# One MoE-plus-state-space layer kernel on one core: order of work in three stages changed

## The reference

```python
xn = layernorm(x)                                   # no gain or offset
# mixer
x_input, x_gate = split(xn @ W_in.T)                # 2 x 1024 channels
u  = silu(conv1d_causal(x_input, conv_w, 4 taps) + conv_b)
Bu = u @ W_B.T                                      # 64 states
h  = scan: h = 0.95 * h + 0.05 * Bu_t               # along each sequence
y  = (h @ W_C.T + D_param * u) * silu(x_gate)
mixer = layernorm(y @ W_out.T + xn) * ln_gamma + ln_beta
# experts: 8 experts, each takes its 1024 rows of highest score
scores = (tanh(xn @ gate_w.T) + 1) * 0.5            # 8192 x 8
vals, idx = top_k(scores.T, 1024)
y = layernorm(xn[idx]) * f_gamma + f_beta
h = gelu_tanh(y @ fc1.T + b1)                       # 2048 wide
o = (h @ fc2.T + b2) * vals
ffn = xn, with o added at the chosen rows
out = x + mixer + ffn
```

## Time and profile before

| | us |
|---|---|
| median of 3 runs | 2889.43 |
| lowest, highest | 2886.38, 2889.5 |
| the profiled execution, device time | 2889.01 |
| its span, first to last instruction | 2887.2 |

### The profile page before, as it was taken

One profiled execution on the slowest core, in us unless ns is written; L12 is line 12 of the kernel. 1 busy time (PEld: TensorE's weight loads), 2 busy tenths in 40 slices (PEclk: granted clock), 3 DMA queues, 4 the chain that ended last, 5 costly groups with the idle time before them and its releaser, 6 DMA issues.

```text
span 2887.2 us, 40293 instructions
## 1 busy us (share of the span) xinstructions
PE 2777.7 (96%) x12168; PEld 2205.1 (76%) x12170; DVE 1854.0 (64%) x3098; ACT 1392.9 (48%) x2325; POOL 659.1 (23%) x1009
## 2 busy tenths in 40 slices
PE   7899999999999999999999999999999999999997
PEld 3478888888887777777777787777877787778776
DVE  7768888888877888878654455545554455445553
ACT  4544555555555565554444444444444444444443
POOL 4422222222222221224221112211221122111211
PEclk9999999999999999999999999999999999999999
DMA  9733322333222223345142131330422214213121
GB/s 330 246 117 102 99 87 90 94 97 95 91 95 92 91 88 103 103 130 186 30 117 60 40 108 31 95 77 13 125 46 73 77 28 111 66 35 112 31 44 15
DMA packets 119193, 265.11 MB, mean 92 GB/s; under 512 B 24208, under 2 KB 24400, under 8 KB 115024
## 3 DMA queue, kind: packets, MB, share of 16 engines
q1 hardware_dynamic: 84752, 164.83, 17.0%
q0 software_dynamic: 34240, 97.85, 14.4%
HBM read 208.86 MB, written 53.77 MB: 91 GB/s over the span
## 4 chain that ended last, share of the span: by engine, by line
PE 84%; DVE 6%; ACT 4%; issue 3%; DMA 2%; POOL 0%; DVEq 0%; SPq 0%; ACTq 0%; POOLq 0%
PE po L1867 8%; PE po L1868 8%; PE po L1869 8%; PE ring L1452 8%; PE ring L1454 8%; PE ring L1453 8%; PE pb L1867 4%; PE pb L1869 4%; PE pb L1868 4%; PE pc L1869 4%; PE pc L1868 4%; PE pc L1867 4%; PE po L1485 3%; PE po L1487 3%; PE po L1486 3%
## 5 line engine op out<-in xcount | busy, mean ns | idle before, releaser
L1867 PE MATMUL po<-w2h,hid_h 128*128 128x512 f32 x1024 | 411.9, 402 | 38.7 <-DVE hid_l L1827 38.6
L1868 PE MATMUL po<-w2l,hid_h 128*128 128x512 f32 x1024 | 407.5, 398 | 0.0
L1869 PE MATMUL po<-w2h,hid_l 128*128 128x512 f32 x1024 | 407.2, 398 | 0.0
L1452 PE MATMUL ring<-xt_h,w_h 128*128 128x512 f32 x1024 | 402.6, 393 | 2.8 <-DVE xt_l L483 2.6
L1454 PE MATMUL ring<-xt_h,w_l 128*128 128x512 f32 x1024 | 401.0, 392 | 0.0
L1453 PE MATMUL ring<-xt_l,w_h 128*128 128x512 f32 x1024 | 398.6, 389 | 0.0
L1254 DVE SCALAR_TENSOR_TENSOR u<-xin,cw,u 128x512 f32<-128x512 f32 x384 | 288.5, 751 | 60.6 <-issue 28.7
L1736 ACT CAST w1h<-w1r 128x512 fp32r<-128x512 f32 x258 | 160.2, 621 | 270.6 <-PE po L1869 261.0
L1715 POOL DMA_INDIRECT out_dram<-res,idx_c x64 | 101.4, 1584 | 820.5 <-DVE res L1851 806.1
L1867 PEld LDWEIGHTS po<-w2h,hid_h 128*128 128x128 f32 x1024 | 195.5, 191 | 92.3 <-DVE hid_l L1827 39.0
L1742 DVE TENSOR_TENSOR w1l<-w1r,w1h 128x512 fp32r<-128x512 f32 x258 | 177.3, 687 | 102.6 <-ACT w1h L1736 78.8
(11 more groups left out here) (206 smaller groups left out, 5774.8 us busy)
## 6 DMA issues: line engine op xcount, KB each, us to landing
wo<-wo_halves POOLq DMA_DIRECT2D x120, 512.0 KB, 4.0
w1r<-fc_in SPq DMA_DIRECT2D x130, 256.0 KB, 2.7
w2r<-fc_in SPq DMA_DIRECT2D x130, 256.0 KB, 2.9
g_x<-x_in SPq DMA_DIRECT2D x16, 1024.0 KB, 7.7
x_tail<-x_in SPq DMA_DIRECT2D x64, 256.0 KB, 2.7
out_dram<-res SPq DMA_DIRECT2D x64, 256.0 KB, 2.1
xt_rows<-g_xnt SPq DMA_DIRECT2D x15, 1024.0 KB, 7.6
rows<-xt_rows SPq DMA_DIRECT2D x15, 1024.0 KB, 5.9
```

The costliest lines, as they stand in the source:

```text
L1452: pe.matmul(ring[r % 2][:, :], w_h[:, r, q], xt_h[:, k, :], start=(k == 0), stop=False)
L1867: pe.matmul(dst, ah, bh, start=start, stop=False)
L1868: pe.matmul(dst, ah, bl, start=False, stop=False)
L1869: return pe.matmul(dst, al, bh, start=False, stop=stop)
```

## The change

- Gate stage: `gv` becomes a view of the tile that later holds the experts' layer-norm gain (512 numbers in each partition, enough for the gate values of all 8192 rows). The 16 stores of 512 rows become one store of all 8192 rows, issued where the last one was, in the mixer's prologue; `gate_values` no longer waits for a store. Waits on 16 stores become waits on one, and SP waits for it before it loads the gain. The semaphores' starts are split: those of the gate stage stand ahead of the loads of blocks 2 and 3, the others behind them.
- Last mixer turn: `sum_rows` of block 15 move into it, each one step behind `normal_rows`; POOL's `twice_scale` moves there too, ahead of the last four loads of `wo`. The load of `b1` moves ahead of weight tile 11 on SP, and DVE copies out its first part ahead of the low weight parts of tile 1. The wait for `b2` moves from ahead of the loop to tile 8 of the first group.
- Experts: `T_AT` becomes (8, 9, 11, 12). ACT runs gelu and `hid_h` ahead of the weights' high parts for every tile; DVE runs `hid_l`, then statistics, then the weights' low parts.

```diff
 def stage_gate(...)
-    gv = m.sb("g_gv", [P, J, E])
+    gv = ew.gamma[:, :].rearrange("p (n e) -> p n e", e=E)
-    gd_v = t["gate_rows"].rearrange("(b j p) e -> b p j e", p=P, j=J)
+    gd_v = t["gate_rows"].rearrange("(n p) e -> p n e", p=P)
     def gate_values(dve, b):
         dve.wait_ge(c_ta, b + 1 + 1)
-        dve.wait_ge(c_gd, 16 * b + 1)
-        dve.tensor_scalar(gv[:, :, :], half_tanh, 1.0, 0.5, ALU.add, ALU.mult).then_inc(c_v, 1)
+        dve.tensor_scalar(gv[:, bass.ds(at(b) * J, J), :], half_tanh, 1.0, 0.5, ALU.add, ALU.mult).then_inc(c_v, 1)
     def end_store(sp):
-        store(sp, NB - 1)
+        sp.wait_ge(c_v, 2 * NB + 1)
+        sp.dma_start(gd_v, gv[:, :, :]).then_inc(c_gd, 16)
     # SP, per block
                 load_x(NB - R + i if last else b + R, i)
-                if not (first and i == 0):
-                    store(sp, b - 1)
                 store_xt(b, i)
         load_x(1, 1)
-        m.counts.start(sp)
+        m.counts.start(sp, sums.counts)
+        m.counts.start(sp, m.counts.counts[begun:own])
         for i in range(2, R):
             load_x(i, i)
+        m.counts.start(sp, m.counts.counts[:begun - len(sums.counts)])
+        m.counts.start(sp, m.counts.counts[own:])
 def stage_mixer(...)
             for i in range(11):
                 expert_tile(b, i)
+            sums.first_bias(sp)
             expert_tile(b, 11)
 ...
+        sp.wait_ge(sums.c_gate_rows, 16 + 1)
         for dst, src in ((ew.gamma, t["f_ln_g"]), (ew.beta, t["f_ln_b"])):
 ...
                 for j in range(J):
                     ew.gather_gates(pool, 0, j)
+                ends.twice_scale(pool, b)
             for c in range(WO, NC_):
                 load_wo(b, c)
 ...
-                act.wait_ge(sums.c_gate_rows, 16 * NB + 1)
+                act.wait_ge(sums.c_gate_rows, 16 + 1)
 ...
                 ends.normal_rows(act, b, k)
+                if last and k >= 1:
+                    ends.sum_rows(act, b, k - 1)
             if last:
                 group_high(KD - 1)
+                ends.sum_rows(act, b, J - 1)
 def stage_experts(...)
-    T_AT = (9, 11, 12, 13)
+    T_AT = (8, 9, 11, 12)
     def first_low(dve, s):
+        if s == 1:
+            dve.wait_ge(c_bias, 16 + 1)
+            bias(dve, 0, 0, 0)
         w_low(dve, s, s)
     # ACT
-        for j in range(J):
-            ends.sum_rows(act, NB - 1, j)
         act.wait_ge(ends.c_po, (NB - 1) * J + 1 + 1)
-                    if s < FT - 1:
-                        next_high(e, i, s)
                     act.wait_ge(c_hl, (g * FT if s < 2 else n - 1) + 1)
                     ...gelu, hid_h...
-                    if s == FT - 1:
-                        next_high(e, i, s)
+                    next_high(e, i, s)
     # DVE
-                    if s < FT - 1:
-                        w_low(dve, n + 2, s + 2)
-                    if 3 <= s < 3 + J:
-                        ew.statistics(dve, g + 1, s - 3)
                     dve.wait_ge(c_hh, n + 1 + 1)
                     ...hid_l...
-                    if s == FT - 1:
-                        w_low(dve, n + 2, s + 2)
+                    if 3 <= s < 3 + J:
+                        ew.statistics(dve, g + 1, s - 3)
+                    w_low(dve, n + 2, s + 2)
                     if 8 <= s < 8 + J:
                         if first and i == 0:
                             dve.wait_ge(ends.c_st[j], 16 * NB + 1)
+                            dve.wait_ge(ew.c_small, 16 * 3 + 1)
-        dve.wait_ge(c_bias, 16 + 1)
-        bias(0, 0, 0)
-        dve.wait_ge(ew.c_small, 16 * 3 + 1)
         pair(0, True)
```

More of the change, by code:

```diff
@@ L32 @@
 HI = CAP // LO
-GATE_GAP = 808
+GATE_GAP = 704
 EXPERT_GAP = 240
@@ L50, in tick, with start @@
         return self.stack.enter_context(self.nc.semaphore(name))
-    def start(self, sp):
-        for c, start in self.counts:
+    def start(self, sp, counts):
+        for c, start in counts:
             sp.sem_inc(c, start)
@@ L200, in __init__ @@
     def __init__(self, m):
+        begun = len(m.counts.counts)
         self.c_in_low = m.count("g_wl")
@@ L216, in __init__ @@
         self.c_list_out = m.count("l_out")
-        self.first_high = self.first_low = None
+        self.counts = m.counts.counts[begun:]
+        self.first_high = self.first_low = self.first_bias = None
 class MixerWeights:
@@ L239, in stage_gate @@
     xnt = [m.sb(f"g_xnt{i}", [P, KD, TB]) for i in range(R)]
-    m.sb("g_gap", [P, GATE_GAP])
-    gv = m.sb("g_gv", [P, J, E])
     stats = m.sb("g_stats", [P, J, 6])
@@ L247, in stage_gate @@
     half = m.sb("g_half", [P, J])
+    gw = m.sb("g_gw", [P, KD, E])
+    m.sb("g_gap", [P, GATE_GAP])
+    gv = ew.gamma[:, :].rearrange("p (n e) -> p n e", e=E)
     sc_t = m.sb("g_sc_t", [E, TB])
     tanh = m.sb("g_tanh", [P, J * E])
-    gw = m.sb("g_gw", [P, KD, E])
     staged2 = m.over("g_staged2", ends.xn_end, J * D * 4, [P, 4, TB])
@@ L256, in stage_gate @@
     w_h, w_l = ew.w1, ew.w2
-    c_id = m.count("g_id")
-    c_gw = m.count("g_gw_in")
-    c_x = [m.count(f"g_x_in{i}") for i in range(R)]
+    begun = len(m.counts.counts)
     c_raw = ends.c_raw
@@ L284, in stage_gate @@
     t_tick = m.tick("g_ttick")
+    c_id = m.count("g_id")
+    c_gw = m.count("g_gw_in")
+    c_x = [m.count(f"g_x_in{i}") for i in range(R)]
+    own = len(m.counts.counts)
     x_v = t["x"].rearrange("(b j p) d -> b p j d", p=P, j=J)
-    gd_v = t["gate_rows"].rearrange("(b j p) e -> b p j e", p=P, j=J)
+    gd_v = t["gate_rows"].rearrange("(n p) e -> p n e", p=P)
     xs_v = t["xt_rows"].rearrange("b p (k n) -> b p k n", k=KD)
@@ L292, in at @@
         return 0 if type(b) is int and b == NB - 1 else b + 1
-    def store(sp, b):
-        sp.wait_ge(c_v, b * 2 + 1 + 1)
-        sp.dma_start(gd_v[at(b)], gv[:, :, :]).then_inc(c_gd, 16)
     def gate_values(dve, b):
         dve.wait_ge(c_ta, b + 1 + 1)
-        dve.wait_ge(c_gd, 16 * b + 1)
         half_tanh = tanh[:, :].rearrange("p (j e) -> p j e", e=E)
-        dve.tensor_scalar(gv[:, :, :], half_tanh, 1.0, 0.5, ALU.add, ALU.mult).then_inc(c_v, 1)
+        dve.tensor_scalar(gv[:, bass.ds(at(b) * J, J), :], half_tanh, 1.0, 0.5, ALU.add, ALU.mult).then_inc(c_v, 1)
         dve.tensor_scalar(gates[:, :, bass.ds(at(b) * J, J)], tanh[:, :].rearrange("p (j e) -> p e j", e=E),
@@ L378, in sync @@
         for i in range(R):
-            store(sp, NB - R + i - 1)
             if i < R - 1:
@@ L1057, in turn @@
                     pool.wait_ge(c_tl, (LAST + 1) * KD + 1)
-                    pool.wait_ge(sums.c_gate_rows, 16 * NB + 1)
+                    pool.wait_ge(sums.c_gate_rows, 16 + 1)
                     ew.take_list(pool, 0, 0)
@@ L1668, in sync @@
     def sync(sp):
-        sp.wait_ge(sums.c_cv, 3 * all_out + 1)
-        sp.wait_ge(sums.c_ho, all_out + 1)
-        sp.dma_start(b1[:, 0:E * FT], t["b1"]).then_inc(c_bias, 16)
         sp.wait_ge(ends.c_o, all_out + 1)
@@ L1720, in gpsimd @@
         pool.wait_ge(sums.c_t, KD + 1)
-        ends.twice_scale(pool, NB - 1)
         for j in range(J):
@@ L1750, in first_low, with bias, first_bias @@
     def first_low(dve, s):
+        if s == 1:
+            dve.wait_ge(c_bias, 16 + 1)
+            bias(dve, 0, 0, 0)
         w_low(dve, s, s)
-    sums.first_high, sums.first_low = first_high, first_low
+    def bias(dve, g, e, i):
+        dve.wait_ge(c_ge, (g - 1) * FT + 1 if type(g) is not int or g else 1)
+        dve.sem_inc(d_tick, 1)
+        dve.tensor_copy(b1c[i][:, :], b1[:, bass.ds(e * FT, FT)]).then_inc(c_b1, 1)
+    def first_bias(sp):
+        sp.wait_ge(sums.c_cv, 3 * all_out + 1)
+        sp.wait_ge(sums.c_ho, all_out + 1)
+        sp.dma_start(b1[:, 0:E * FT], t["b1"]).then_inc(c_bias, 16)
+    sums.first_high, sums.first_low, sums.first_bias = first_high, first_low, first_bias
     def scalar(act):
@@ L1802, in keep @@
             ew.keep(dve, g, i)
[L1804 to L1807, removed]
         def tail(s):
@@ L1836, in pair @@
                         keep(g + 1, 1 - i)
-                        bias(g + 1, e + i, 1 - i)
+                        bias(dve, g + 1, e + i, 1 - i)
                     if 8 <= s < 8 + J:
@@ L1853, in pair @@
                                              op0=ALU.mult, op1=ALU.add).then_inc(c_rw, 1)
-        dve.wait_ge(c_pad, 1 + 1)
-        dve.wait_ge(c_bias, 16 + 1)
-        bias(0, 0, 0)
         for j in range(J):
             ends.take(dve, NB - 1, j)
-        dve.wait_ge(ew.c_small, 16 * 3 + 1)
+        dve.wait_ge(c_pad, 1 + 1)
         pair(0, True)
@@ L1943, in build @@
         ends = RowEnds(m, t, banks)
+        ew = Experts(m, t, ends)
         sums = Between(m)
-        ew = Experts(m, t, ends)
         with ExitStack() as small:
```

## The result

The changed kernel takes 2825.35 us (median, 2824.57 to 2826.88) beside 2889.47 us (2886.38 to 2891.33) for the kernel before: a ratio of 0.978, 95% interval 0.9763 to 0.9797. The profiled execution takes 2825.14 us, its span is 2823.4 us instead of 2887.2. The forecast of 2828 us was 2.7 us too high.

What follows compares the result with a forecast made beforehand. PE, busy 96% of the span, was taken as the bound, so only its waits and slow clock could be won: 2889.0 - 34.7 (group ends) - 13.7 (clock) - 2.45 (loop heads) - 3.8 (seam) - 6.2 (gate stage) = 2828 us, range 2820 to 2843.

Steps and rivals of the forecast that it cites:

- Group ends: Experts: gelu(15) queues behind the last slice's t_high; with that moved, PE's 16 waits for hid_l go, 34.7 us.
- Clock: Experts: low granted clock follows PE waits of 2.0 us or more; 13.7 us come back, bounds 0 and 13.7.
- Rival (C): Experts: the clock still falls behind group ends or elsewhere; 2842 us, chance 0.13.
- Loop heads: Head of an expert loop pass: the table load falls into ACT's idle time and six small PE waits go, 2.45 us.
- rival (B): Head of an expert loop pass: the table load stands behind gelu's wait; 2837 us, chance 0.12.
- Seam: From mixer to experts: ACT's shorter entry gives -2.1 us net, the clock -1.7; sum -3.8 us, bounds 0 and -5.
- Gate stage: Gate stage: ten blocks without store waits give -5.0 us, the earlier start -1.2; sum -6.2 us, bounds -2 and -11.5.
- Rival (A): Gate stage: DMA bounds it at 364 GB/s, ten blocks take 65 us; 2830 us, chance 0.66 together with the forecast.
- The weight parts: Experts: weight parts come later, with 4.1 us of cover left, 1.3 us at group heads; costed at nothing.
- (D): Experts' group ends: gelu(15) stays late because ACT has tile 16's weight casts before it; 2876 us, chance 0.05.
- (E): Gate-row store: the one store takes 96 us and holds PE up 67 us; 2895 us, chance 0.04 with similar slowdowns.

Runs made afterwards that it cites:

- experiment 1: The kernel before with only T_AT changed to (8, 9, 11, 12): 2842.47 us, ratio 0.9833.
- experiment 2: The changed kernel with T_AT back at (9, 11, 12, 13): 2870.76 us, ratio 0.9933.
- experiment 10: The changed kernel with gate rows stored block by block again from the large tile, DVE waiting for no store: 2823.77 us, ratio 0.9773.
- experiment 8: The changed kernel with gelu's wait for hidden(s) put first of its three waits, not last: 2835.24 us, ratio 0.9814.
- experiment 3: The kernel before with only the new order of ACT and DVE inside an expert tile: 2878.02 us, ratio 0.9954.
- experiment 4: The changed kernel with the old order of ACT and DVE inside an expert tile: 2835.25 us, ratio 0.9807.

## Why the prediction was right, point by point

- **Group ends: right in mechanism, 1.6 us small.** The theory stands by experiments 1 and 2, which put in and take out one line. The term of 16 x 2.17 left out the 0.10 us by which the second matmul is late; with 2.01 + 0.26 it is 36.3 us.
- **Clock: right, and at the upper bound.** Eight low stretches behind group ends are gone, and that at the start of the stage. Rival (C), that the clock falls by itself, is out for the experts: no stretch is left there in the changed kernel. Elsewhere too a wait of PE stands beside each. The stretch near 120 us, in 6 of the 13 traces, comes at PE's wait of 2.6 us for `xt_l` as the mixer begins; that near 200 us, in 6 of 13 as well (before and after among them), comes at a wait of 1.5 us for `u_l` in mixer turn 0. First the matmul and its window in experiment 10, then in the changed kernel:

```profile
118.54 0.75 PE L1466 MATMUL ring<-xt_h,w_h 128*128 128x512 f32 x1 [2.58 <-DVE xt_l L491]
118.00:123.00 5.00, 4.46 (x12) 3.33 (x12) 0.50 (x2) 0.00 (x0) 0.00 (x0) 0.66 0.81 297
...
192.89 0.80 PE L1491 MATMUL po<-wo,u_h 128*128 128x512 f32 x1 [1.50 <-DVE u_l L1295]
192.00:197.00 5.00, 4.11 (x11) 3.33 (x12) 4.55 (x12) 3.21 (x6) 1.32 (x2) 0.66 0.65 210
```

  The same waits stand in the other traces without a low stretch, so each of these comes and goes between kernels that are equal there, and is worth 1.7 us.
- **Loop heads: right in mechanism, too small.** I took 2.45 us from the brackets and had corrected the same kind of bracket at the group ends a paragraph before. Six waits with 0.26 us more each are 4.0 us; the experts' 55.1 us less 36.3 and 9 x 1.7 leave 3.5. The reading that the load falls ahead of the last wait was right; experiment 8 shows that rival (B) was one line away.
- **Seam: -3.8 expected, -3.3 found (1.6 + 1.7 of clock), with two errors that nearly cancel.** The start of hidden(0) moved by 1363.37 - 1357.64 = 5.7 us, so of the gate stage's 7.06 us it lost 1.3, not 0.7. The wait before out_share(0) is 1.05 us, as 1.4 were expected, so 2.9 us came back there instead of 2.8. Experiments 3 and 4 show that this gain belongs to the new order (2.0 to 2.3 us), not to the work moved into the mixer. Without the order (experiment 4) the way from PE's first matmul of the mixer to out_share(0) takes 1368.61 - 118.83 = 1249.8 us, 1.7 of it for one more low stretch; before the change it took 1373.24 - 126.01 = 1247.2. The moved work gained nothing there by itself.
- **Gate stage: -6.2 expected, -7.1 found.** The ten blocks took the 63.2 us of the sum, to 0.1 us. The start gave 25.77 - 24.20 = 1.6 us instead of 1.2, and the blocks behind the ten another 0.5, which no term held. Rival (A) is out with the price that it had: it took 364 GB/s as the rate of the DMA and so 65 us for the ten blocks. DVE waits 2.4 us for x in that stretch, but with the stores' waits gone the same ten blocks moved faster than 364. The windows of the ten blocks, before and after:

```profile
25.77:93.99 68.22, 58.46 (x281) 26.86 (x280) 55.38 (x140) 32.40 (x71) 35.72 (x70) 1.00 1.03 360
24.20:87.42 63.22, 58.92 (x282) 26.96 (x281) 57.95 (x140) 32.77 (x71) 35.16 (x70) 1.00 1.02 378
```

  A DMA share of 1.0 stood in both, so it did not show a bound. Whether DMA bounds the stage at its new rate is open: PE and DVE are busy for 93% and 92% of that window, so a faster PE or DVE alone would probably win little (argued, not tried).
- **The weight parts: right.** No PE wait for `w1l` or `w2l` in 16 groups; the cover of 1.3 us at the heads was enough.
- **(D) and (E): out.** gelu(15) is on time in every group, since PE waits at none; the store landed in 7.6 us, not in 29 to 96. My bounds for it multiplied the landing time by the rows: 16 times the rows took 4.2 times the 1.8 us of the store that was issued alone.

Term by term (group ends, loop heads by what is left of the experts, seam, gate stage) the errors are +1.6, +1.0, -0.5 and +0.9, together 3.0 us. The terms of the sum are 60.85 us and the span fell by 63.8, 2.95 more; the median came out 2.7 us below the forecast. So the forecast is not right by luck of large errors that cancel; its one term that could have been anything from 0 up was the clock, which was taken at its upper bound.

## What to carry to other kernels

Where a late last step (here one transposed slice) queues ahead of the activation that feeds the busiest engine, move the step, not the engine's work: one tuple brought three quarters of the gain, and part of it was clock. Price a wait of TensorE by the interval between matmul starts on both sides of it, not by its bracket, and price those of about 1.9 us or more with their share of low clock. Before an activation that needs a new table, put the wait that ends last behind its other waits.

## What the runs showed of the hardware

- The granted clock in the experts behind a wait of PE: never low behind 0.2 to 1.6 us; low behind 1.87 us in 4 of 8 cases, behind 2.0 us in 8 of 16 (before), 6 of 16 (experiment 2) and 7 of 17 (experiment 3), behind 2.29 us in 8 of 16, and at each of 3.33, 3.98 and 4.01 us. With 2.29 us it came behind every second group end, always the one that ends the first half of a pass.
- The length of the wait does not decide alone. In mixer turn 0 the second of two waits of 1.5 us, 9 us apart, had a low stretch in 6 of 13 traces, and the wait of 2.6 us at the mixer's start in 6 of 13. What decides between equal waits stays open. All 50 low stretches of the 13 traces, up to the end of PE's work, begin within 2 us of the end of a PE wait of about 1.5 us or more; none stands by itself.
- A low stretch is 3.4 us long and costs 1.7 us, but for two of 6.8 us in experiment 1, at waits of 3.03 us (84.78) and 3.98 us (1375.92).
- A table load of 1.28 us is issued ahead of the wait that stands last before its activation (changed kernel) and behind one that stands first of two (rows 12) or of three (experiment 8); the next activation begins 1.29 us after the load does.
- 8192 rows of 32 bytes in one store landed in 7.6 us, while stores of 512 such rows took 1.8 to 9.0 us: the time does not grow in step with the rows. The traffic beside these stores was not the same.
